# Forty turns of the identity in the first two rounds of tempered attention's measuring loop

## The reference, cut to what matters

```python
qk = jnp.einsum('bhqd,bhkd->bhqk', Q, K)
scores = qk / math.sqrt(dk)
mean_sim = scores.mean(axis=(-2, -1))
max_sim = scores.max(axis=-1).mean(axis=-1)
probs = jax.nn.softmax(scores, axis=-1)
entropy_proxy = jnp.var(probs, axis=-1, ddof=1).mean(axis=-1)
feats = jnp.stack([mean_sim, max_sim, entropy_proxy], axis=-1)
...                                   # three linear layers give log_t
attn_scores = qk / (2.0 * jnp.exp(log_t)[..., None])
attn = jax.nn.softmax(attn_scores, axis=-1)
```

## Time and profile before

| what | value |
|---|---|
| median of three runs | 1165.21 us (1164.88 to 1170.04) |
| profiled execution, its own time | 1170.82 us |
| its span, first to last instruction | 1168.8 us |
| TensorE busy (PE) | 950.2 us, 81% |
| VectorE busy (DVE) | 737.8 us, 63% |
| ScalarE busy (ACT) | 583.5 us, 50% |
| GpSimd busy (POOL) | 414.3 us, 35% |
| mean granted TensorE clock | 0.896 |

### The profile page before, as it was taken

One profiled execution on the slowest core, in us unless ns is written; L12 is line 12 of the kernel. 1 busy time (PEld: TensorE's weight loads), 2 busy tenths in 40 slices (PEclk: granted clock), 3 DMA queues, 4 the chain that ended last, 5 costly groups with the idle time before them and its releaser, 6 DMA issues. The chain is left out here.

```text
span 1168.8 us, 26585 instructions
## 1 busy us (share of the span) xinstructions
PE 950.2 (81%) x10747; PEld 626.4 (54%) x10777; DVE 737.8 (63%) x2034; ACT 583.5 (50%) x956; POOL 414.3 (35%) x426
## 2 busy tenths in 40 slices
PE   4999898999999977988897690886657686579997
PEld 2677433443333424777676390555446475447776
DVE  3587776547656464653575044379899999646754
ACT  3365565545555425643662550476545645325542
POOL 4320300000000012777001656146678877623340
PEclk9799899999999988998897795988688878699998
DMA  7000000000000007000000322100000000000001
GB/s 272 1 3 2 20 1 1 1 1 0 1 0 1 0 21 279 3 3 2 2 3 1 92 65 65 55 1 1 1 3 3 2 3 3 1 2 2 3 2 37
DMA packets 15432, 27.93 MB, mean 24 GB/s; under 512 B 1104, under 2 KB 13264, under 8 KB 14544
## 3 DMA queue, kind: packets, MB, share of 16 engines
q1 hardware_dynamic: 14288, 24.14, 5.8%
q0 software_dynamic: 1024, 2.10, 0.6%
HBM read 20.33 MB, written 5.90 MB: 22 GB/s over the span
## 5 line engine op out<-in xcount | busy, mean ns | idle before, releaser
L1333 PE MATMUL l0f_ctl<-l1f_in,l0f_in 128*128 128x512 f32 x320 | 145.5, 598 | 0.4
L133 POOL TENSOR_SCALAR row_var_eps<-row_mean_var 128x12 f32<-128x12 f32 (+2 forms) x16 | 3.6, 223 | 352.9 <-DVE row_mean_var L128 352.1
L556 DVE TENSOR_REDUCE l_neg_max<-l_ring 128x4 f32<-128x512 f32 x128 | 82.1, 684 | 63.3 <-PE l_ring L418 62.7
L515 ACT ACTIVATE l_probs<-l_scores 128x1024 f32<-128x1024 f32 x64 | 65.6, 1025 | 82.2 <-PE l_scores L426 82.2
L2690 ACT COPY l2f_blocks_sb<-l2f_right_t_sb 32x1024 f32<-32x1024 f32 x64 | 66.8, 1044 | 66.1 <-PE l2f_given_ps L2620 39.5
L1333 PEld LDWEIGHTS l0f_ctl<-l1f_in,l0f_in 128*128 128x128 f32 x320 | 61.4, 192 | 70.6 <-issue 69.1
L2620 PE MATMUL l2f_given_ps<-l2f_blocks_sb,l2f_left_t_sb 128*32 128x128 f32 x1024 | 47.7, 363 | 34.2 <-ACT l1f_in L2696 23.8
L706 POOL TENSOR_TENSOR l_squares<-l_exps 128x1024 f32<-128x1024 f32 x32 | 60.6, 1895 | 29.7 <-ACT l_exps L961 29.7
L2620 PEld LDWEIGHTS l2f_given_ps<-l2f_blocks_sb,l2f_left_t_sb 128*32 128x32 f32 x1024 | 41.8, 148 | 48.3 <-issue 47.8
L1053 DVE TENSOR_REDUCE l_neg_max<-l_scores 128x8 f32<-128x1024 f32 x32 | 39.2, 1225 | 43.1 <-PE l_scores L758 43.1
L376 POOL TENSOR_SCALAR_AFFINE_SELECT l_probs<-l_probs 128x1024 f32<-128x1024 f32 x32 | 35.0, 1094 | 62.3 <-ACT l_probs L515 62.3
(11 more groups left out here) (460 smaller groups left out, 2621.8 us busy)
## 6 DMA issues: line engine op xcount, KB each, us to landing
l1f_in<-in_l1f SPq DMA_DIRECT2D x1, 4580.0 KB, 13.6
l0f_in<-in_l0f SPq DMA_DIRECT2D x1, 2302.5 KB, 8.9
l0f_in<-in_l2f SPq DMA_DIRECT2D x1, 2080.5 KB, 18.7
l1f_in<-in_l2u SPq DMA_DIRECT2D x1, 2048.0 KB, 9.0
sorted_rows<-first_in SPq DMA_DIRECT2D x1, 1856.0 KB, 11.0
l1f_sorted<-sorted_rows SPq DMA_DIRECT2D x7, 256.0 KB, 5.2
expert_rows<-l1f_sorted SPq DMA_DIRECT2D x7, 256.0 KB, 2.2
x_in<-in_x SPq DMA_DIRECT2D x1, 1024.0 KB, 4.8
```

Source lines behind the costliest of these rows:

```text
L515: nc.scalar.activation(probs[c % 2][:, 2 * pair:2 * pair + 2], scores2[:, :, :, :, :], ACT.Exp, scale=SCORE_SCALE).then_inc(exp_done, 1)
L556: ring.free(V.tensor_reduce(out, score_bank(b, half, g), AX.X, ALU.max, negate=True), ("score", b, half, g))
L1333: return nc.tensor.matmul(out, lhs, rhs, start=start, stop=stop)
```

## The change

A new function turns the identity with the identity, so many times, into one place of a bank. In `measure`, in rounds 0 and 1 (both halves), TensorE first waits that the last rows of `xnT` are copied, and then issues ten such turns into `scores2[:, 0, 0, 0, :]`, ahead of its own waits. That makes 40 transposes 128x128. Nothing reads what they write. No semaphore is added, and no other engine's program changes.

```diff
@@ -213,6 +213,12 @@
         ins.then_inc(self.xnT_stored, 1)
         if i == 0:
             self.normalise_on_act(11)
+
+
+def turn_identity(nc, m, room, times):
+
+    for _ in range(times):
+        nc.tensor.transpose(room, m["identity"][:, :], m["identity"][:, :])
 
 
 def first_layernorm(nc, m, tag, meanwhile):
@@ -737,6 +743,9 @@
             def measure(b, c, half):
                 first, second = exists(b), exists(c)
                 pair1, pair2 = half, 1 - half
+                if b < 2:
+                    norm.wait_stored(pe, NCH - 1)
+                    turn_identity(nc, m, scores2[:, 0, 0, 0, :], 10)
                 if first:
                     pe.wait_ge(stored, KINDS * (b // 4) + KINDS)
                     if 2 * b + half:
```

## The result

The changed kernel took 1176.97 us, the median of six runs (1170.88 to 1178.17), against 1165.24 us (1163.4 to 1171.83, six runs) for the kernel before: 1.0074 times as long, with a 95% interval from 1.0047 to 1.0102. I had forecast 1168.0 us and a range up to 1172.2. A second comparison on another occasion, with 12 and 35 runs, gave 1174.61 against 1166.96 us, 1.0061 (1.0040 to 1.0082). By these ratios the change costs 8.6 and 7.1 us, with intervals from 5.5 to 11.9 and from 4.7 to 9.6, and not 2.8.

The account below looks back on a forecast made before the run. Rounds 0 and 1 were taken as bound by one chain of TensorE scores and VectorE maxima. 4 x 1.18 = 4.70, less cover of 0.48, 1.18 and 0.24, gave +2.8: 1165.21 + 2.82 = 1168.0 us, range 1163.3 to 1172.2.

Parts of the forecast that it names:

- The price of a turn: Each added transpose on TensorE takes 0.1175 us at full clock, 1.18 us for ten; 0.242 each at half clock.
- The four groups: Ten turns ahead of each half of rounds 0 and 1: shifts 1.18, 1.88, 1.88, 2.82 us.
- the second group: Turns ahead of half 1 of round 0: no gap covers them, plus 1.18, shift 1.88 us.
- the fourth: Turns ahead of half 1 of round 1: a gap of 0.24 covers part, plus 0.94, shift 2.82 us.
- The added wait: Ahead of the first half, turns wait for ScalarE's last copy of `xnT`: about nothing, or 0.1 to 0.3 us.
- The clock in these rounds: Low clock near round 2 recurs unchanged, 2.8 us later: term taken as 0, bounds 0 and -1.39 us.
- My rival of +1.4 us: Turns make rounds 0 and 1 dense, the low stretch near round 2 goes: 2.82 - 1.39, 1166.6 us; 30 in 100.
- The step that failed: TensorE's delay at round 2, 2.82 us, passes on in full through the layer and the next.
- gains and losses of later layers from the clock: Fewer low stretches behind the change could give 6 us or more, 1158 us, 5 in 100; the opposite as likely.
- The rule on transposes: Transposes may not count as TensorE being busy for the clock; then the low stretch stays, 2.8 us or more.
- turns that count as idling: Turns act as holes for the clock, which falls again inside rounds 0 and 1: +4.5, 1169.7 us; 12 in 100.
- The spread: Runs of the kernel before differ by 5.16 us; 0.5%, 5.8 us, is about what a measurement can tell.

Follow-up runs that it names:

- five turns: Changed kernel with five turns for each half in place of ten: 1171.95 us, 1.0017 against the kernel before.
- turns in the two covered gaps: Kernel before plus ten turns ahead of the first halves of rounds 1 and 2 only: 1171.21 against 1168.07 us, ratio 1.0006.
- twenty turns: Changed kernel with twenty turns for each half in place of ten: 1176.06 us, 1.0045 against the kernel before.
- ten matmuls: Changed kernel with ordinary 128x128 identity matmuls in place of the turns, same places and number: 1176.36 us, 1.0071 against the kernel before.
- turns ahead of round 2 too: Changed kernel plus ten turns ahead of the first half of round 2: 1172.47 us, 1.0035 against the kernel before.
- maxima in rounds 0 and 1: Kernel before, no turns, three extra VectorE maxima delaying the halves of rounds 0 and 1: 1174.41 us, 1.0058.
- 0.7 ahead of the pass: Kernel before plus an unused 0.68 us VectorE maximum just ahead of the tempered pass (scores of L845): 1168.96 us, 0.9987.
- 1.2 ahead of the pass: Kernel before plus an unused 1.23 us VectorE maximum just ahead of the tempered pass: 1172.18 us, 1.0032.
- 1.9 ahead of the pass: Kernel before plus unused VectorE maxima of 1.23 + 0.68 us just ahead of the tempered pass: 1171.57 us, 1.0045.
- 2.5 ahead of the pass: Kernel before plus unused VectorE maxima of 2 x 1.23 us just ahead of the tempered pass: 1173.5 us, 1.0053.
- the covered turns: Kernel before plus ten turns only in gaps where TensorE waits: ahead of round 1 (1168.7 us, 0.9987), or of rounds 1 and 2 (1171.21 us, 1.0006).
- the long rows: 120 turns, or 120 matmuls, in one row at the start of the layer's TensorE program; one execution each, no total time given.

## Why the prediction was wrong

- **The price of a turn** (0.1175 us) was right: 0.12 measured. I took the clock as high in all these microseconds, where the earlier trace rows show it only from 457 to 458; it was so.
- **The four groups** were right in place and order, 2.54 us in the trace against 2.82. The difference is 0.14 us less at the second group and 0.16 less at the fourth.
- **The added wait** costs nothing, as forecast: the first half is 1.20 us late with ten turns of 1.21 ahead of it.
- **The clock in these rounds** I took as unchanged; in both traces of the changed kernel the low stretch near round 2 is gone. My rival of +1.4 us was right on that and wrong on the total. The filling isn't the whole reason: the stretch is gone too with five turns, with turns ahead of round 2 as well and with turns in the two covered gaps, but it is there with twenty turns and with ten matmuls, which fill the same places longer. What it gave back doesn't show: from round 2 to the loop's last scores of `scores2`, the changed kernel takes 87.7 us (463.5 to 551.2) and 88.1 (462.2 to 550.3), and the kernel before 89.2 (457.4 to 546.6) and 87.4 (458.7 to 546.1).
- **The step that failed** is the one on what lies behind: "The whole layer is one such chain, and the next layer starts from its end, so I take a delay of TensorE at round 2 as passed on in full." For the changed kernel that is wrong: its total grows by 8.6 and 7.1 us where round 2 is 2.5 late. The table sets the delay in each trace beside the total, both in us; the total is the ratio's.

| kernel | delay in trace | total (interval) | pass in trace |
|---|---|---|---|
| changed, first | 2.54 | 8.6 (5.5 to 11.9) | 59.4 |
| changed, again | 2.55 | 7.1 (4.7 to 9.6) | 58.5 |
| turns ahead of round 2 too | 2.54 | 4.1 (1.3 to 6.9) | 59.5 |
| maxima in rounds 0 and 1 | 5.00 | 6.8 (4.2 to 9.3) | 59.5 |
| 0.7 ahead of the pass | 0.60 | -1.5 (-4.8 to 1.9) | 58.5 |
| 1.2 ahead of the pass | 1.14 | 3.7 (0.4 to 7.1) | 58.5 |
| 1.9 ahead of the pass | 1.73 | 5.3 (2.0 to 8.5) | 60.1 |
| 2.5 ahead of the pass | 2.26 | 6.2 (3.2 to 9.2) | 58.3 |
| five turns | 0.91 | 2.0 (-0.9 to 4.9) | 56.4 |
| twenty turns | 6.67 | 5.3 (2.0 to 8.4) | 56.3 |
| ten matmuls | 6.95 | 8.3 (5.1 to 11.6) | 56.2 |

Something on top of the delay is clear of noise in the changed kernel, twice, and in the kernel that idles 2.5 us with no turn in it, and barely with 1.9; elsewhere the delay alone would do. So the turns aren't needed for it. Where it goes is told by the traces and is less sure. The pass grows by 2.0 to 3.8 us in eight traces of seven kernels, the upper eight rows. It stays at 55.8 to 56.4 in the other nine, among them both of the kernel before, the covered turns and the long rows. Over the pass PEclk is 0.85 to 0.89 in all eight and 0.93 or 0.94 in all nine, so the longer pass is one at a lower clock. In the upper eight rows the total exceeds the delay by 2.7 us on the mean, in the lower three by 0.4, which fits, though single rows run from -2.1 to 6.1. I had written that gains and losses of later layers from the clock are equally likely and had put them in the tails; the term that I put at nothing came out as a loss of 4.5 to 6 us for this kernel.

- **The rule on transposes.** I gave 12 in 100 to turns that count as idling, leaning on the trace of an earlier layer. The Trainium skill (page "TensorE: Matmul & The Clock Gate", section "Part 4: PE-mode transpose") says that the full clock doesn't engage for transposes. The row of 120 turns, one trace, speaks against it for f32 128x128, at 5.9 us for both kinds; the measurement decides.
- **The spread.** I took 5.16 us from three runs for the kernel's spread. With 35 runs it is 13 to 22 us from end to end, and the median of the kernel before lies between 1165.24 and 1168.86 us on five occasions. The 5.8 us that I took as what a measurement can tell from no change was far too sure for three runs.

**What stays open.** Of the 7 us or more, 2.5 are turns and 2.2 to 3.1 are the longer pass in the changed kernel's two traces. The other 2 us or so I can't place: most kernels have one trace, and its other stages differ between traces of the same kernel by as much. Nor is it shown that the kernel decides whether the pass is long: the two kernels with two traces each repeat theirs, but one trace is one of executions that differ by 10 us. Why a pass that starts later keeps the low clock longer, and why the traces of five and twenty turns escape it, is seen only as where the clock comes back. I found no cause behind that.

## What to carry to other kernels

Fill with warming work only the time that TensorE waits through anyway; ten turns in a gap of 1.42 us were free, and ten with no gap cost their 1.2 us. All forty cost 2.5 us in place, more than the 1.4 of the low stretch that they could prevent. A delay of a few microseconds ahead of stages at half clock may cost more than its length, here 4.5 us or more on top of 2.5; it needn't, as five and twenty turns show. Look at granted clock stage by stage before and after, not at its mean (0.896 and 0.897 here). And when single executions differ by 10 us, a median of a few runs can't size a change of 3.

## What the runs showed of the hardware

- Turns of the identity (f32, 128x128) are spaced 0.11 us at full clock inside a long row (82 of them start from 446.8 to 455.6 us), and ten take 1.18 to 1.21 us to the work behind them. They brought up the clock as soon as matmuls did, 5.9 us into a row for both, in one trace of each.
- An f32 matmul 128x128 with 128 columns leaves two records, 240 for 120 matmuls in 29.85 us, against 16.16 us for 120 turns, the first 5.9 us of each at half clock.
- With gaps of 1.03 and then 2.54 us between the halves in place of turns, the clock fell to half at about 454 us, between the two gaps, and was still there at 466; with turns it held through both rounds.
- The same pass of 512 score matmuls took 55.8 to 56.4 us at a mean granted clock of 0.93 or 0.94, and 58.3 to 60.1 at 0.85 to 0.89 (17 traces).
